# Macaron block: layout of the convolution's first spectrum, LayerNorm statistics, bias rows and load order changed

## What is computed

```python
def _layernorm(x, axis=-1, eps=1e-5):
    m = jnp.mean(x, axis=axis, keepdims=True)
    v = jnp.var(x, axis=axis, keepdims=True)
    return (x - m) / jnp.sqrt(v + eps)
# attn(x, t): FFT convolution along the sequence, n = 8192 positions, filter t of 4096, L = 2n
    xf = jnp.fft.rfft(x, n=L, axis=1);  tf = jnp.fft.rfft(t, n=L, axis=0)
    y = jnp.fft.irfft(xf * tf[None], n=L, axis=1)[:, :n, :]
# ffn(x): DIM = 1024, HIDDEN = 3072, int32 weights times 1/127
    gate = einsum('bsd,hd->bsh', x, wg); up = einsum('bsd,hd->bsh', x, wu)
    return einsum('bsh,dh->bsd', silu(gate) * up, wd)
# the layer; x is (8, 8192, 1024) f32
    x = x + 0.5 * ffn(_layernorm(x));  x = x + attn(_layernorm(x), t);  x = x + 0.5 * ffn(_layernorm(x))
```

## Time and profile before

| | us |
|---|---|
| median of 3 runs | 8928.23 |
| lowest and highest | 8908.58, 9134.22 |
| the profiled execution | 8907.92 |
| its span on the slowest core (core 4) | 8905.9 |
| span of the 8 cores | 8825.4 to 8905.9 |
| PE, DVE, ACT busy in that span | 6836.0, 3368.5, 2186.5 |
| ACT_TABLE_LOAD in the whole run | 1 |

### The profile page before, as it was taken

One profiled execution on the slowest core, in us unless ns is written; L12 is line 12 of the kernel. 1 busy time (PEld: TensorE's weight loads), 2 busy tenths in 40 slices (PEclk: granted clock), 3 DMA queues, 4 the chain that ended last, 5 costly groups with the idle time before them and its releaser, 6 DMA issues.

```text
span 8905.9 us, 133195 instructions; the slowest of 8 cores (8825.4 to 8905.9 us)
## 1 busy us (share of the span) xinstructions
PE 6836.0 (77%) x42236; PEld 3497.6 (39%) x42648; DVE 3368.5 (38%) x5181; ACT 2186.5 (25%) x2737; POOL 74.6 (1%) x101
## 2 busy tenths in 40 slices
PE   2455358898889889883776666676799899899899
PEld 1343313333333333332566555566233333333333
DVE  2555313323322332225666666666222222222222
ACT  2555201111111111114433544433111111111111
POOL 0000000000000000000000000000000000000000
PEclk9666679999999999995566655566899999999999
DMA  7522563443334334423011011011443343443443
GB/s 112 85 53 51 146 151 71 89 92 84 80 87 94 75 82 94 92 63 73 30 39 37 18 39 37 27 39 44 101 103 93 95 104 88 100 104 83 104 103 80
DMA packets 1810144, 699.23 MB, mean 79 GB/s; under 512 B 1712288, under 2 KB 1745344, under 8 KB 1805856
## 3 DMA queue, kind: packets, MB, share of 16 engines
q1 hardware_dynamic: 947024, 402.83, 16.9%
q10 hardware_dynamic: 798720, 201.38, 10.0%
q0 software_dynamic: 63760, 86.48, 6.5%
HBM read 617.42 MB, written 138.51 MB: 85 GB/s over the span
## 4 chain that ended last, share of the span: by engine, by line
PE 60%; DVE 17%; DMA 9%; ACT 5%; issue 4%; another core or an unknown queue 2%; SPq 1%; DVEq 1%; ACTq 0%; POOL 0%; POOLq 0%
PE pb L880 15%; PE pb L895 14%; PE pb L936 8%; PE pbf L936 7%; DVE p2B L83 4%; DVE t_B L83 4%; DVE f1rows L83 3%; DMA f3wgT<-s_wgT 3%; PE pb L876 3%; PE pb L891 3%; ACT p2win L83 2%; PE pb L634 2%; PE pb L639 2%; PE pb L602 2%
## 5 line engine op out<-in xcount | busy, mean ns | idle before, releaser
L880 PE MATMUL pb<-f1lnsl,f1wgT 128*128 128x512 bf16 x3008 | 809.4, 390 | 224.7 <-DMA f1wgT<-s_wgT 190.9
L880 PE MATMUL pb<-f3lnsl,f3wgT 128*128 128x512 bf16 x2995 | 804.6, 390 | 175.7 <-DMA f3wgT<-s_wgT 144.0
L83 DVE TENSOR_TENSOR f3hid<-f3silu,pb 128x512 bf16<-128x512 bf16 x384 | 264.1, 688 | 1580.8 <-ACT f3silu L83 1575.4
L895 PE MATMUL pb<-f3lnsl,f3wuT 128*128 128x512 bf16 x3009 | 790.6, 383 | 4.8 <-issue 2.4
L83 DVE TENSOR_TENSOR f1hid<-f1silu,pb 128x512 bf16<-128x512 bf16 x384 | 264.0, 688 | 1398.1 <-ACT f1silu L83 1389.2
L895 PE MATMUL pb<-f1lnsl,f1wuT 128*128 128x512 bf16 x2992 | 784.9, 382 | 3.4
L83 ACT CAST p2B<-pb 128x512 bf16<-128x512 f32 (+1 forms) x512 | 548.6, 1071 | 503.3 <-PE pb L608 466.1
L83 ACT ACTIVATE f1silu<-pb 128x512 bf16<-128x512 f32 x384 | 229.5, 598 | 1730.7 <-PE pb L895 1432.9
L83 DVE CAST p2B<-pb 128x512 bf16<-128x512 f32 (+1 forms) x512 | 577.3, 1127 | 184.4 <-PE pb L608 144.7
L83 ACT ACTIVATE f3silu<-pb 128x512 bf16<-128x512 f32 x384 | 229.4, 597 | 1641.5 <-PE pb L895 1547.1
L413 PE MATMUL pb<-f1sb,t_win 32*64 32x130 bf16 x2048 | 239.7, 334 | 434.7 <-DMA t_win<-t 263.2
(11 more groups left out here) (122 smaller groups left out, 8247.8 us busy)
## 6 DMA issues: line engine op xcount, KB each, us to landing
f1wuT<-s_wuT ACTq DMA_DIRECT2D x384, 256.0 KB, 3.2
f1wgT<-s_wgT SPq DMA_DIRECT2D x384, 256.0 KB, 3.2
f3wuT<-s_wuT ACTq DMA_DIRECT2D x384, 256.0 KB, 3.2
f3wgT<-s_wgT SPq DMA_DIRECT2D x384, 256.0 KB, 3.2
out<-f3res SPq DMA_DIRECT2D x16, 2048.0 KB, 11.3
s_that<-t_thre SPq DMA_DIRECT2D x64, 256.0 KB, 2.0
s_that<-t_thim SPq DMA_DIRECT2D x64, 256.0 KB, 2.4
f1xsl<-xT POOLq DMA_DIRECT2D x16, 1024.0 KB, 13.8
```

The source lines that it names most:

```text
L83: ins = attr(*a, **kw)
L880: rec.add("tensor", lambda t, c=c, sl=sl, q=q: t.matmul(pg[q][:, 0:SB], wgT[:, sl * NCH * P + c * P:sl * NCH * P + (c + 1) * P], lnsl[i % ...
L895: rec.add("tensor", lambda t, c=c, sl=sl, q=q: t.matmul(pu[q][:, 0:SB], wuT[:, sl * NCH * P + c * P:sl * NCH * P + (c + 1) * P], lnsl[i % ...
```

## The change

One diff with several parts:

1. **Bias rows.** `gsum`, `usum`, their 384 matmuls in p0a and all matmuls of lines 876 and 891 go. `prologue_b` broadcasts both rows (factor and offset) and VectorE adds the offset after the multiplication, 8 more additions of 128x512 per block.
2. **Inverse square root.** `rowmath` and `row2` become: Square on ScalarE, two VectorE instructions, Sqrt on ScalarE, then `reciprocal` and one or two more on VectorE. Engines alternate through semaphores.
3. **Layout of `B`**: `p (c rk)`. Stage 1's eviction writes 130 elements side by side per channel; stage 2's moving operand becomes `Bv[:, :, br*65+bc]`, 128 elements with a step of 130.
4. **p0b loads.** The three casts are issued first of all; `t_win` gets two buffers, and the load of group g waits for stage 1 of group g-2; waits for constants are split by constant.
5. **Transposes of p2.** One instruction on all 128 partitions evicts a pair, in turn on ScalarE and VectorE; factor and offset are rearranged once (`r2m`, `b2m`).
6. **Engines.** `ptw` of every fourth `jb` runs on GpSimd; of the evictions of lines 602/608 VectorE keeps one in four, ScalarE has three.

```diff
+            if "p0a" in self.phases:
+                for k in "gud":
+                    self.p0a_casts(k)
             self.conv_consts_load()
             self.p0b()
...
             for l in (0, 1):
                 rec.add("gpsimd", lambda gg, l=l, g=g: gg.dma_start(
                     out=winv[64 * l:64 * l + 32, :, :],
                     in_=tin[l, :, :, g * P:(g + 1) * P]),
-                    waits=[("winfree" + sfx, rec.n("winfree" + sfx))],
-                    incs=[("winld" + sfx, 16)])
+                    waits=[(s_s1, max(0, rec.n(s_s1) - 64))],
+                    incs=[(wsem, 16)])
...
+                if jj % 2 == 0:
+                    rec.add("scalar", lambda s, jj=jj, pt=pt: s.activation(
+                        winv[:, jj, :], pt[:, :], AF.Identity,
+                        bias=b2n[:, jj:jj + 1], scale=r2n[:, jj:jj + 1]),
...
-        Bv = B.rearrange("p (r k c) -> p r k c", r=2, k=65)
+        Bv = B.rearrange("p (c rk) -> p c rk", c=P)
...
-                pin = pin.rearrange("p ci (r k) -> p ci r k", r=2)
-                ov = Bv[:, :, :, 2 * ch2:2 * ch2 + 2].transpose([0, 3, 1, 2])
+                ov = Bv[:, 2 * ch2:2 * ch2 + 2, 0:130]
...
-                        gv[:, gs, k2, :], Bv[:, br, bc, :],
+                        gv[:, gs, k2, :], Bv[:, :, br * 65 + bc],
...
-                rec.add("vector", ptw,
+                rec.add("gpsimd" if jb % 4 == 3 else "vector", ptw,
...
-                rec.add("vector" if cp % 2 == 0 else "scalar", i1ev,
+                rec.add("vector" if cp % 4 == 0 else "scalar", i1ev,
...
+            rec.add("scalar", lambda s: s.activation(
+                rowf[0:1, 3 * SB:4 * SB], pstat[0:1, 0:SB], AF.Square),
+                waits=[(T("std"), rec.n(T("std"))), (T("rowq"), rec.n(T("rowq")))],
+                incs=[(T("rowsq"), 1)])
+            def rowq(v):
+                q = rowf[0:1, 3 * SB:4 * SB]
+                v.scalar_tensor_tensor(q, q, -1.0 / DIM, pstat2[0:1, 0:SB],
                                        ALU.mult, ALU.add)
...
+                return v.tensor_scalar(q, q, 1.0 / DIM, EPS, ALU.mult, ALU.add)
...
+            rec.add("scalar", lambda s: s.activation(
+                rowf[0:1, 0:SB], rowf[0:1, 3 * SB:4 * SB], AF.Sqrt),
...
+            def rowb(v):
+                v.reciprocal(rowf[0:1, 0:SB], rowf[0:1, 0:SB])
+                v.tensor_copy(rows_bf[0:1, 0:SB], rowf[0:1, 0:SB])
+                return v.scalar_tensor_tensor(rows_bf[0:1, SB:2 * SB], pstat[0:1, 0:SB],
+                                              -1.0 / DIM, rowf[0:1, 0:SB],
                                               ALU.mult, ALU.mult)
...
+                def lnap(v, bi=bi, xs=xs, c=c):
+                    v.tensor_mul(lnsl[bi][:, c * SB:(c + 1) * SB],
+                                 xsl[xs][:, c * SB:(c + 1) * SB], rbp[:, 0:SB])
+                    return v.tensor_add(lnsl[bi][:, c * SB:(c + 1) * SB],
+                                        lnsl[bi][:, c * SB:(c + 1) * SB], rbp[:, SB:2 * SB])
...
-                    if c == NCH - 1:
-                        rec.add("tensor", lambda t, ht=ht, q=q: t.matmul(
-                            pg[q][:, 0:SB], self.gsum[0:1, ht * P:(ht + 1) * P],
-                            rows_bf[0:1, SB:2 * SB], start=False, stop=False,
-                            skip_group_check=True))
```

More of the change, by code:

```diff
@@ L496, in conv_group @@
                 w0 = [(s_s1e, s1e_total)]
+                if mode == "t" and jb == 0 and jq == 0:
+                    w0.append(("cc_g", self.cc_tgt["g"]))
                 rot = "xev" + sfx if mode == "x" else s_ptw
@@ L576, in conv_group @@
         if mode == "t":
-            rec.add("sync", lambda sy: sy.nop(), waits=[(s_s1, rec.n(s_s1))],
-                    incs=[("winfree" + sfx, 1)])
             return
@@ L689, in p0b @@
         for g in range(NGRP):
-            if "p0a" in self.phases and g in (1, 2, 3):
-                self.p0a_casts("gud"[g - 1])
+            bufs["win"] = wins[g % 2]
             self.conv_group(g, "t", bufs)
@@ L787, in prologue @@
             xs = i % nxs
-            lw = [("wsumev", 12 if "p0a" in self.phases else 0)]
+            lw = []
             if i == 0:
@@ L808, in prologue @@
                    ("cst", 32), (T("l2row"), rec.n(T("l2row")))]
-            if "p0a" in self.phases:
-                stw.append(("wsumev", 12))
             for c in range(NCH):
@@ L1012, in down_store, with l2b @@
+                def l2b(v):
+                    v.reciprocal(rowf[0:1, SB:2 * SB], rowf[0:1, SB:2 * SB])
+                    return v.scalar_tensor_tensor(
+                        rowf[0:1, 2 * SB:3 * SB], pstat[0:1, 0:SB],
+                        -1.0 / DIM, rowf[0:1, SB:2 * SB], ALU.mult, ALU.mult)
+                rec.add("vector", l2b,
+                        waits=[(T("l2r"), rec.n(T("l2r")))],
                         incs=[(T("l2row"), 1)])
                 rec.add("sync", lambda sy, i=i: sy.dma_start(
-                    out=self.s_ln2[0:1, i * SB:(i + 1) * SB], in_=rows[0:1, 2 * SB:3 * SB]),
```

234 lines of the change are left out of this document (100 added, 134 removed).

## The result

The changed kernel takes 8223 us (undisturbed runs 8213.0 to 8223.3) against 8895.8 to 8930.9 in the four fastest runs before: a ratio of 0.922, with an interval of 0.919 to 0.926.

The account below looks back on a forecast made before the run. TensorE bounds the FFN phases, evictions bound stage 1, other convolution stages vary. Filter -72, signal -307 and FFN -483 make -862 on 8908: 8046 us, own range 7840 to 8270, 8-in-10 range 7640 to 8490.

Parts of the forecast that it names:

- Bias matmuls: FFN blocks: removing 48 one-row matmuls per block, each priced at 0.216 us, saves 332 us.
- f1's third tile: f1 blocks: a shorter row chain frees SP earlier, TensorE's idle time falls to about 3 us; -152 us.
- f3's stall: f3's third tile: the 2 MB result store still sets when weights arrive, TensorE comes 0.9 us earlier; +14 us.
- Transposes: Signal groups: 32 ScalarE evictions on 128 partitions set the length, 37.7 to 19.5 us, -18.2 a group.
- Stage 1: Convolution groups: contiguous evictions of about 430 ns cut it from 54.8 to 21 us (filter), 56 to 22 (signal).
- Stage 2: Convolution groups: the strided moving operand makes it 62 us (55 to 70), +25.6 per filter group, +19.7 per signal group.
- the rival of streams that take turns: Stage 2: the strided streams alternate, 213 ns a matmul, stage 109 us; total 8798 us; chance 0.15.
- the slower one: Stage 2: streams take turns at the contended rate, 274 ns a matmul, stage 140 us; total 9294 us; chance 0.05.
- the first rival: Stage 2: the moving operand pays nothing for its step, stage stays 36.4 and 42.3 us; total 7683 us; chance 0.22.
- T = 5: Signal's stage 2: GpSimd's six product instructions for every fourth jb take 5 us, covered up to 7.8; tail 12.9 to 7.
- Casts and gaps: Filter phase: casts ahead of everything on POOL cost +140 us (105 to 170); shrinking gaps between groups return -146.
- The three widenings: Forecast range 7935 to 8174 widened for stage 1 (+-4 x 16), casts and f1's stall (+-35 each).

Follow-up runs that it names:

- the two runs on the bias matmuls: Kernel before with the matmuls of lines 876 and 891 removed (8678.7 us), or given 128 contraction rows (8967.2 us); kernel before at best 9038 us there.
- The combined kernel: Also "the last kernel": changed kernel plus waits once, five-frequency blocks of B, VectorE products, casts between groups, stores on POOL; 7596.8 and 7647.1 us.

## Why the prediction was right or wrong

The direction, the mechanism of stage 2, and the range held; the total of 8046 was 177 us too low, as the sum of two larger misses of opposite sign. That 8223 lies inside the forecast's own 7840 to 8270 is therefore luck: FFN 211 us better, convolution and what lies before f1 389 us worse (rounded terms: -480 against -691, -382 against +7).

- **Bias matmuls: -332 predicted, -650 measured.** The step that failed is the price of 0.216 us for a 512-column matmul. It was read in a dense stretch of 128-row matmuls and carried to one-row ones. The tile pitch in the trace of before had the answer: 4.300 us for 18 matmuls, where 18 x 0.216 is 3.89. The 0.41 us that are left over were there to be asked for; the two runs on the bias matmuls put them on the row count.
- **f1's third tile: -152 predicted, -70 measured.** The idle time that the gate weights' DMA ends fell from 190.9 us to 120.8 in the 16 blocks (in seven other executions with the same f1 it is 81 to 104, so the term is known to some 40 us only). The row chain became nearly as short as expected although the reciprocal took 3.34 us instead of 2 (my upper bound was 3.1): `row2`'s start to the issue of the gate weights took 17.4 us before and takes 8.2. What failed is the last term, a weight load of about 3.6 us, and TensorE's arrival. The timeline of one boundary:

```profile
2277.09 3.34 DVE L82 RECIPROCAL f1rowf<-f1rowf 1x512 f32<-1x512 f32 x1 [1.00 <-ACT f1rowf L82]
2281.30 0.21 SPq L1003 DMA_DIRECT2D s_ln<-f1rowf  x1
2282.20 9.23 SPq L762 DMA_DIRECT2D f1wgT<-s_wgT  x3
2287.26 3.57 PE L872 MATMUL pb<-f1lnsl,f1wgT 128*128 128x512 bf16 x8 [6.45 <-DMA f1wgT<-s_wgT]
```

  From the issue at 2282.20 to the matmul it is 5.1 us. TensorE arrives 7.1 us after the boundary instead of 8.8, so 1.7 us earlier and not 0.9, since its tiles fell by more than was counted. The idle time is 5.4 to 12.7 us, not 3. The trace shows what the earlier issue ran into: the load of the next block's x, which landed at 2445.67 before, 9 us ahead of the gate weights' issue, and now lands about with it or later. Where it lands up to 2 us after the issue the idle time is 5.4 to 6.7 us; where 3 to 6, 7.8 to 10.0; where about 8, 12.4 and 12.7. What makes even the quick loads 5.1 us was not tested.
- **f3's stall: +14 predicted, -4 measured** (144.0 to 140.2 us of idle time ended by the gate weights; seven other executions with the same f3 have 139 to 163, so these 4 us say nothing of the sign). The combined kernel left the stall where the weights come over another queue; it is the store and the x load beside it, and not the store alone as the prediction had it, that hold back the weights.
- **A term that was missing:** the sums of the second matmul group in the statistics (line 817, now 809) take a mean of 555 ns and 579 ns instead of 448 and 432, and the eight of a block a mean of 3.2 us from first start to last end instead of 2.3: some +28 us. It is the granted clock: where it is 1.0 throughout the eight take 1.89 us, at 0.5 they take 3.57, and over them it is 0.84 and 0.86 in the mean before (f1, f3), 0.64 and 0.59 after. TensorE has been idle for 3.45 us ahead of them in both kernels, behind ScalarE's work on `lnsl`; why the clock falls more often now was not tested. With it the FFN adds up: -650 - 70 - 4 + 28 = -696 of -691.
- **Table loads: nothing, as predicted.** 64 loads of 1.28 us, 82 us of ScalarE, do not show in the tile pitch.
- **Transposes: -18.2 a group predicted, 0 measured (146 us in all).** The step by which ScalarE's evictions set the stage was wrong: ScalarE's 29 us of 37.7 are near but not full, and TensorE's five waits a pair set it. The evictions of 128 partitions cost 463 ns, as said.
- **Stage 1: 21 and 22 predicted, 31.3 and 39.4 measured (221 us in all).** The evictions are as predicted (428 against 430 ns, and VectorE waits for TensorE). TensorE's "about 0.25 us x 64 = 16" counted weight loads and matmuls alone. Without the repeated waits the stage is 20 us, so that term was 4 us too small for the instructions and lacked the waits' 0.11 us each.
- **Stage 2: 62 predicted, 59.4 measured in all 16 groups.** The bounds of 55 to 70 from the strided weight loads held: 1.81 ns a column in place of 1.7. In the trace the next pair starts 230 ns after the one before it. A lone matmul with the same step and columns, the one between stage 1 and stage 2, takes 388 ns from start to end where it took 266 with its operand side by side. Those 122 ns for one stream are what a pair takes longer (230 against 107 ns at the same, half clock); if the streams of a pair took turns, one alone would need only about half. The semaphore that this matmul raises says the same: it comes 402 ns after the start at this step of 260 bytes, 316 at the 10 bytes of the last kernel, and 280 side by side. So the two streams run at once, each slowed by its own lines. Before, then after:

```profile
L437 PE MATMUL pb<-p2B,misc 128*1 128x128 bf16 x8 | 2.1, 266 | 19.3 <-DVE p2B L83 17.0 <-ACT p2B L83 2.3
L416 PE MATMUL pb<-p2B,misc 128*1 128x128 bf16 x8 | 3.1, 388 | 7.8 <-ACT p2B L82 7.8
```

  That settles the rival of streams that take turns and the slower one; the first rival (no price for the step) falls with it. The Trainium skill (TensorE: Matmul & The Clock Gate, Part 2) has one read port for the moving operand of a standard matmul, and the same part gives matmuls on two column halves more interfaces ("column tiling 2×/4×" uses 4/8); the prediction left the second out, and this trace agrees with it.
- **GpSimd: T = 5 predicted, 6.9 measured** (6 x 1.15 to 1.20 us), below the 7.8 from which it would decide. The tail is 10.0 and not 7, +24 us, and the move as a whole costs 58: VectorE's products beside it take 482 to 619 ns instead of 425 (425 again in the kernel without it), and it has the last product of a group. As an edit by itself it should not have been made.
- **Casts and gaps: +140 and -146 predicted, +155 and -151 measured** (167 us of gaps and final tail became 741.2 - 8 x 90.7 = 16). Both as told.
- **The width of the range.** The three widenings (64, 35 and 35 us) were put together as 95; their plain sum is 134. 8223 lies inside by either.

The sum of the convolution's misses: 146 + 221 + 24 + 15 - 5 - 16 x 2.6 = 359 of the 389; the rest is in the weights and first loads (201.6 us, 8 more than before and 11 more than predicted) and in differences between groups that one group's rows don't show.

Of the signs named ahead, the starts of line 509 (490 after), its stage near 62 us, the evictions near 430 ns and the first stage 1 near 240 us came in; stage 1 near 21, the third tile's 3 us and GpSimd's instructions under 1 us did not; the blocks, foreseen near 158 us, were 151.4 and 145.3.

## What to carry to other kernels

Before a stage is costed by its busiest engine, divide its length by its repetitions and check that the instructions account for the pitch; what is left over (0.41 us in a tile here, 0.3 us in a pair of transposes) is a cost of its own, and it was the largest term in both misses. Satisfied waits in TensorE's program cost 0.11 us each once they outlast the instructions beside them (here the fourth and fifth), so wait once for what stays true. A layout need not choose between a cheap write and a cheap read: count the 16-byte lines that a strided read touches, at 1.8 ns each, and check what else holds the stage. A shorter chain lets a transfer start earlier, and into whatever is then in flight: look for that before its idle time is counted as saved.

## What the runs showed of the hardware that was not expected

- A satisfied semaphore wait on TensorE costs 0.11 us in a stream of short instructions when there are four or five before each group (29.6 to 36.6 us for 64 more), and hides beside the instructions when there are two (0.33 us a pair, 0.31 with about one); it appears as idle time with the cause "issue".
- A one-row matmul between 128-row ones costs 0.424 us, a 128-row one of the same 512 columns 0.216; its weight load and the next one's start with their matmuls instead of 0.21 us ahead.
- A strided moving operand costs 1.8 ns for each 16-byte line that it touches, at either level of the clock: a pair of 128-column matmuls takes 117, 144, 228 and 230 ns at steps of 8, 10, 16 and 260 bytes. Two such streams on different columns of the array run at once.
- VectorE's reciprocal of 512 float32 elements on one partition takes 3341 ns, more per element (6.5 ns) than the scattered evictions (6.0).
- A 2 MB store and a 1 MB load delay weight loads of other queues as much as those of their own: 144.0 and 140.2 us of idle time before f3's gate weights, 166.8 before its up weights when the store is moved from SP to POOL.
